# Sparse attention and slot experts on one core: GpSimd lowers the scores of batch 0 one group later and ends the new threshold, and ScalarE's sign passes follow

## The reference

```python
def sparsemax(z):
    z_sorted = -jnp.sort(-z, axis=-1)
    cum = jnp.cumsum(z_sorted, axis=-1)
    k = jnp.arange(1, S + 1, dtype=z.dtype)
    support = 1.0 + k * z_sorted > cum
    k_sup = jnp.sum(support, axis=-1, keepdims=True)
    cum_sel = jnp.take_along_axis(cum, k_sup - 1, axis=-1)
    tau = (cum_sel - 1.0) / k_sup
    return jnp.maximum(z - tau, 0.0)
```

## Time and profile before

| | us |
|---|---|
| median of 3 runs | 485.32 (484.76 to 485.77) |
| the profiled execution | 485.12 |
| its span | 483.4 |
| VectorE busy | 313.0 (65%) |
| TensorE busy | 400.4 (83%) |
| ScalarE busy | 225.9 (47%) |
| GpSimd busy | 149.1 (31%) |

### The profile page before, as it was taken

One profiled execution on the slowest core, in us unless ns is written; L12 is line 12 of the kernel. 1 busy time (PEld: TensorE's weight loads), 2 busy tenths in 40 slices (PEclk: granted clock), 3 DMA queues, 4 the chain that ended last, 5 costly groups with the idle time before them and its releaser, 6 DMA issues. The chain is left out here.

```text
span 483.4 us, 6967 instructions
## 1 busy us (share of the span) xinstructions
PE 400.4 (83%) x2091; PEld 248.0 (51%) x2091; DVE 313.0 (65%) x1189; ACT 225.9 (47%) x412; POOL 149.1 (31%) x243
## 2 busy tenths in 40 slices
PE   3886576778897987997888998999997659999983
PEld 3543223234454554565656775734443326888872
DVE  3699999978999986675214244333332214989996
ACT  2226647646686796788434654200000001346671
POOL 3105645554858523333111110010000000335453
PEclk9997888788999998999997999999999799999998
DMA  4294011010010128458228757649999999901125
GB/s 148 86 296 131 10 44 43 1 43 27 19 43 2 62 103 298 130 182 295 90 87 301 264 176 241 255 140 392 392 395 394 393 379 356 356 5 45 55 77 174
DMA packets 44030, 83.78 MB, mean 173 GB/s; under 512 B 1878, under 2 KB 36316, under 8 KB 39388
## 3 DMA queue, kind: packets, MB, share of 16 engines
q1 hardware_dynamic: 42936, 82.15, 48.3%
q10 hardware_dynamic: 1060, 1.22, 0.8%
HBM read 70.78 MB, written 12.58 MB: 172 GB/s over the span
## 5 line engine op out<-in xcount | busy, mean ns | idle before, releaser
L1071 PE MATMUL bank<-Wz,yT 128*128 128x512 f32 x128 | 70.8, 706 | 25.9 <-DVE top L1649 23.3
L1071 PEld LDWEIGHTS bank<-Wz,yT 128*128 128x128 f32 x128 | 28.0, 228 | 61.5 <-issue 50.3
L1649 DVE MAX8 top<-bank 128x8 f32<-128x32 f32 x512 | 51.5, 180 | 1.9 <-ACT arena L746 1.7
L1007 ACT ACTIVATE d<-d 128x32 f32<-128x32 f32 x16 | 3.7, 230 | 89.4 <-DVE d L2029 89.4
L579 POOL TENSOR_SCALAR veps<-mv 128x4 f32<-128x4 f32 x24 | 5.9, 244 | 108.8 <-DVE mv L1577 76.4
L1104 PE MATMUL bank<-aWo,hoT 128*128 128x256 f32 x128 | 37.0, 413 | 0.1
L687 POOL TENSOR_TENSOR work<-work 128x512 f32<-128x512 f32 x16 | 16.6, 1058 | 64.7 <-DVE work L2104 64.7
L1138 PE MATMUL bank<-arena,Wd 128*128 128x512 f32 x64 | 29.2, 599 | 3.2 <-ACT arena L809 3.2
L1167 PE MATMUL bank<-d,work 128*128 128x256 f32 x128 | 30.6, 385 | 0.9 <-ACT d L837 0.9
L1509 PE MATMUL bank<-scr,work 128*128 128x256 f32 x128 | 29.1, 381 | 1.6 <-ACT work L1020 1.6
L1485 PE MATMUL bank<-scr,arena 128*128 128x256 f32 x128 | 28.9, 381 | 0.0
(11 more groups left out here) (267 smaller groups left out, 880.3 us busy)
## 6 DMA issues: line engine op xcount, KB each, us to landing
arena<-in_L_ffn_e_W_dram SPq DMA_DIRECT2D x10, 1024.0 KB, 7.8
x<-in_L_ffn_e_W_dram SPq DMA_DIRECT2D x9, 1024.0 KB, 9.4
arena<-in_L_ffn_e_Wg_dram SPq DMA_DIRECT2D x7, 1024.0 KB, 11.3
scr<-in_L_ffn_e_W_dram SPq DMA_DIRECT2D x7, 1024.0 KB, 13.8
work<-in_L_ffn_e_W_dram SPq DMA_DIRECT2D x5, 1024.0 KB, 14.0
xin<-in_L_attn_query_dram SPq DMA_DIRECT2D x8, 512.0 KB, 4.1
x<-in_L_attn_query_dram SPq DMA_DIRECT2D x1, 4096.0 KB, 16.5
out_dram<-x SPq DMA_DIRECT2D x8, 512.0 KB, 5.5
```

What stands on the lines that cost most here:

```text
L1071: mm = pe.matmul(bZ[t % 2][:, :], yT[:, c, t * P:(t + 1) * P], Wz[:, c, :], start=(c == 0), stop=(c == C - 1))
L1649: mx = v.max(top[:, h * TG + t, :], bZ[t % 2][:, h * NS:(h + 1) * NS])
```

## The change

- GpSimd: `lower(i)` of batch 0 moves behind `subtract(i+1)` (the last one stays behind `new_threshold(3)`). A new GpSimd function `new_threshold` does exc - 1 when the sum is there, multiplies it with VectorE's reciprocal and adds `tau`: three 128x64 instructions. VectorE's L1698 and L1704 go in batch 0. Two of the three steps replace those, the third is the split of a combined one.
- VectorE waits for `tau_ready` before it overwrites `tau` (L1663).
- ScalarE: `signs(i)` moves one group later, to the place behind `clamp(i+1)` and `mark(i+1)`; it writes to `unread`, a free stretch of `arena`, and no longer to `above`. The order behind it is now `put_scores(i+1, 2:4)`, `norm_y(i+2)`, `put_yT(i+2)`, `put_scores(i+2, 0:2)`: `norm_y` has changed places with `put_scores(i+1, 2:4)`.
- TensorE's, SyncE's orders and batch 1 are as before, apart from counted semaphore values.

```diff
--- before.py
+++ after.py
@@ -133,6 +133,7 @@
         y = sb("y", [P, TG, D])
         yT = sb("yT", [P, C, GT])
         d = sb("d", [P, TG * 512])
+        unread = arena[:, 12288:13312].bitcast(BF16)
         above = sb("above", [P, TG * 512], BF16)
         top = sb("top", [P, HR, TOP])
         tau = sb("tau", [P, HR])
@@ -256,6 +257,7 @@
         found = sem("found")
         fix = sem("fix")
         tau_ready = sem("tau_ready")
+        risen = sem("risen")
         lowered = sem("lowered")
         signed = sem("signed")
         settled = sem("settled")
@@ -327,6 +329,7 @@
         psH = bank[6][:, 0:D]
         psO = bank[7][:, 0:D]
         N_W2, N_W3 = 7, 3
+        NW = 6
 
         (M_MISC, M_AQ, M_KQ, M_WZ, M_DK, M_DQ, M_V, M_WD) = range(1, 9)
         PREP = M_WD
@@ -596,7 +599,8 @@
 
             def lower(i, b):
 
-                hold(tau_ready, i + 1)
+                pool.wait_ge(tau_ready, i + 1)
+                pool.nop(nofuse=True)
                 z3 = scr[b][:, :, bass.ds(i * TG - b * KT, TG), :]
                 pool.tensor_tensor(z3, z3, tauf[:, :].rearrange("p (h t) -> p h t", h=NH).unsqueeze(3)
                                    .broadcast_to([P, NH, TG, NS]), ALU.subtract).then_inc(lowered, 1)
@@ -611,6 +615,16 @@
                                        tau[:, :].rearrange("p (h t) -> p h t", h=NH)[:, h, :].unsqueeze(3)
                                        .broadcast_to([P, NH // 2, TG, NS]), ALU.subtract).then_inc(diff, 1)
 
+            def new_threshold(i):
+
+                hold(newton, i * (NW - 1) + 1)
+                pool.tensor_scalar(tauf[:, :], exc[:, :], -1.0, None, ALU.add).then_inc(risen, 1)
+                hold(newton, i * (NW - 1) + 4)
+                pool.wait_ge(risen, i * 2 + 1)
+                pool.tensor_tensor(tauf[:, :], tauf[:, :], rcnt[:, :], ALU.mult).then_inc(risen, 1)
+                pool.wait_ge(risen, i * 2 + 2)
+                pool.tensor_tensor(tauf[:, :], tau[:, :], tauf[:, :], ALU.add).then_inc(tau_ready, 1)
+
             def slot_root(b):
                 pool.wait_ge(smean, 2 * b + 2)
                 pool.tensor_scalar(sveps[:, :], smv[:, 1:2], EPS, None, ALU.add).then_inc(srst, 1)
@@ -619,12 +633,14 @@
 
             roots(0, 0)
             roots(0, 1)
-            with pool.Fori(0, GB - 1) as i:
+            subtract(0, 0)
+            roots(0, 2)
+            new_threshold(0)
+            with pool.Fori(1, GB) as i:
                 subtract(i, 0)
+                lower(i - 1, 0)
                 roots(0, i + 2)
-                lower(i, 0)
-            subtract(GB - 1, 0)
-            roots(0, GB + 1)
+                new_threshold(i)
             lower(GB - 1, 0)
 
             pool.wait_ge(dve_part, PREP)
@@ -766,7 +782,7 @@
             def signs(i, b):
 
                 act.wait_ge(lowered, i + 1)
-                act.activation(above[:, :].rearrange("p (h t s) -> p h t s", h=NH, t=TG),
+                act.activation((unread if b == 0 else above)[:, :].rearrange("p (h t s) -> p h t s", h=NH, t=TG),
                                scr[b][:, :, bass.ds(i * TG - b * KT, TG), :], ACT.Sign, bias=tiny[:, 0:1],
                                accum_out=ahead[:, bass.ds(i, 1)]).then_inc(signed, 1)
 
@@ -844,26 +860,21 @@
             put_scores(0, 0, range(TG))
             put_yT(1)
             put_scores(1, 0, range(2))
-            with act.Fori(0, GB - 2) as i:
+            for i in range(GB - 1):
                 clamp(i)
                 mark(i)
+                if i > 0:
+                    signs(i - 1, 0)
+                put_scores(i + 1, 0, range(2, TG))
                 norm_y(i + 2)
-                put_scores(i + 1, 0, range(2, TG))
                 put_yT(i + 2)
-                put_scores(i + 2, 0, range(2))
-                signs(i, 0)
-            clamp(2)
-            mark(2)
-            norm_y(4)
-            put_scores(3, 0, range(2, TG))
-            put_yT(4)
-            put_scores(4, 1, range(2))
-            signs(2, 0)
+                put_scores(i + 2, (i + 2) // GB, range(2))
 
             clamp(3)
             mark(3)
+            signs(2, 0)
+            put_scores(4, 1, range(2, TG))
             norm_y(5)
-            put_scores(4, 1, range(2, TG))
             put_yT(5)
             signs(3, 0)
             put_scores(5, 1, range(2))
@@ -1660,13 +1671,16 @@
                                        in1=rk[:, :].unsqueeze(1).broadcast_to([P, HR, TOP]),
                                        op0=ALU.add, op1=ALU.mult).then_inc(cum, 1)
                 v.wait_ge(cum, i * 3 + 2)
+                if not (isinstance(i, int) and i in (0, GB + 1, GB + 2, GB + 3)):
+
+                    v.wait_ge(tau_ready, i)
                 v.tensor_reduce(tau[:, :], top[:, :, :], AX_X, ALU.max).then_inc(cum, 1)
 
             def scores_at(i, b):
                 return scr[b][:, :, bass.ds(i * TG - b * KT, TG), :]
 
             def steps_ahead(i, b):
-                return i * NW if b == 0 else GB * NW + (i - GB) * (NW + 1)
+                return i * (NW - 1) if b == 0 else GB * (NW - 1) + (i - GB) * (NW + 1)
 
             def count(i, b, marks):
 
@@ -1688,12 +1702,14 @@
                 v.wait_ge(folded, 2 * i + 2)
                 v.tensor_reduce(cnt[:, :], a2[:, :, 0:NS // 4], AX_X, ALU.add).then_inc(newton, 1)
 
-            def new_threshold(i, at):
+            def new_threshold(i, at, by_pool=False):
 
                 v.wait_ge(newton, at)
                 v.tensor_scalar(cnt[:, :], cnt[:, :], 1.0, None, ALU.max).then_inc(newton, 1)
                 v.wait_ge(newton, at + 1)
                 v.reciprocal(rcnt[:, :], cnt[:, :]).then_inc(newton, 1)
+                if by_pool:
+                    return
                 v.wait_ge(newton, at + 2)
                 v.scalar_tensor_tensor(out=rcnt[:, :], in0=exc[:, :], scalar=-1.0, in1=rcnt[:, :],
                                        op0=ALU.add, op1=ALU.mult).then_inc(newton, 1)
@@ -1705,7 +1721,7 @@
 
             def settle(i, b, marks):
 
-                new_threshold(i, steps_ahead(i, b) + (2 if marks else 3))
+                new_threshold(i, steps_ahead(i, b) + (2 if marks else 3), by_pool=marks)
                 v.tensor_reduce(tot[:, 0, bass.ds(i - b * GB, 1)], cnt[:, :], AX_X, ALU.add).then_inc(newton, 1)
 
             def half_rows(a, u):
@@ -1738,7 +1754,7 @@
             def check(b):
 
                 n = GB + b
-                v.wait_ge(newton, steps_ahead(GB * (b + 1) - 1, b) + NW + b)
+                v.wait_ge(newton, steps_ahead(GB * (b + 1) - 1, b) + (NW - 1, NW + 1)[b])
                 v.wait_ge(signed, GB * (b + 1) + b)
                 if b == 0:
                     v.tensor_scalar(tot[:, 1, 0:GB], ahead[:, 0:GB], float(HR * NS), 0.5, ALU.add, ALU.mult)\
@@ -1910,7 +1926,6 @@
                     v.tensor_copy(hidT[:, :, b, :], bZ[1][:, 32:64].rearrange("p (c e) -> p c e", c=C)).then_inc(dve_part, 1)
                     v.wait_ge(slots, s0 + NSL)
 
-            NW = 6
             NSL = 8
             first_statistics(1)
             v.wait_ge(bo_in, 32)
```

## The result

The changed kernel takes 492.75 us (median of 4 runs, 492.43 to 494.31) against 485.04 (4 runs, 484.53 to 485.77). The ratio is 1.0163, 95% interval 1.0141 to 1.0185: 7.7 us or 1.6% slower. Forecast were 487.0 and a range up to 489.6, so the sign was right, the size too small by a factor of four, and the time lies outside the range. The profiled execution took 492.43, its span is 490.7.

A forecast was written before the change was run, and what follows sets the result against it. VectorE bounds batch 0 before; afterwards a ScalarE-TensorE loop of 11.88 + D does. The last pair ends at 88.08 + 4D = 107.88 against 106.09, 1.8 us later: 487.0 us, range 484.6 to 489.6.

The forecast's parts named there:

- The chain: Batch 0, ScalarE and TensorE: serial steps from one group's clamp to the next, last pair 1.8 us later.
- closing pair D: TensorE, a group's last score products, for the next group but one: 4.95 us each, bounds 3.70 and 6.54.
- the turn: TensorE's turn of y between norm_y and put_yT, taken from 80.15 to 81.38 us.
- What bounds the kernel: Before the change, batch 0 goes at VectorE's pace; the last score pair's end, 106.09 us, releases batch 1 through the check.
- VectorE's part: VectorE in batch 0: 0.52 us a group saved by dropping L1698 and L1704, scan 0.32 shorter in groups 0 to 2.
- The fold: VectorE's fold, groups 1 to 3: waits 0.4 us for GpSimd's lowering, taking back the scan's 0.32.
- GpSimd's three instructions: GpSimd's 128x64 threshold steps in batch 0: 0.25 us each, hidden beside VectorE's sort.
- The loop 11.88 + D: ScalarE and TensorE, clamp to clamp in batch 0: 11.88 us plus the closing score pair, 16.83 us in all.
- The bound: TensorE's upper limit for a closing pair: 6.54 us, taken as a pair wholly at half clock.
- 88.08: Batch 0: the fixed part, in us, of the forecast end of the last closing pair, 88.08 + 4D = 107.88.
- Granted clock over batch 0: TensorE's granted clock in batch 0: would be lower than 0.80.
- Late xin: Load of xin lands at 54.2 us in group 0, against group 1's statistics wanted at about 53.3; 0.9 late once.

The follow-up runs named there:

- experiment 11: Changed kernel with VectorE's last two threshold steps (L1698, L1704) back and GpSimd's three small instructions out in batch 0: 493.28 us, ratio 1.0197 to the kernel before.
- experiment 12: Kernel before with only norm_y(i+2) moved behind the copies of put_scores(i+1, 2:4) in ScalarE's order: 493.50 us, ratio 1.0197.
- experiment 1: Changed kernel with ScalarE's sign pass moved from behind the mark to behind put_yT: 487.82 us, ratio 1.0058 to the kernel before.
- experiment 3: Changed kernel with 16 idle products ahead of each turn of y in batch 0 and 4 behind it: 484.20 us, ratio 0.9987 to the kernel before.
- experiment 2: Changed kernel with sign pass behind put_yT, norm_y directly behind the mark and GpSimd's roots ahead of the lowering: 488.44 us, ratio 1.0068 to the kernel before.
- experiment 4: Kernel before with only the new threshold's last steps moved to GpSimd, L1698 and L1704 out of VectorE: 483.93 us, ratio 0.9996.

## Why the prediction was wrong in size

The chain was the right one, and the sign came out by it and not by luck. The step that failed is TensorE's part of the chain: the closing pair D was taken at 4.95 us and took 6.00 on average, and the turn was taken at full clock, 1.23 us, and took 1.98 three times in four. Point by point:

- **What bounds the kernel, and that the end of the last closing pair is the number to follow**: right. Flag minus pair end was 2.39 before and 2.38 after; the pair's end moved by 7.2 and the span by 7.3.
- **VectorE's part**: right. 0.52 us a group (L1725 at 64.16, 0.47 behind the reciprocal), scans of 1.22, 1.23, 1.22, and one of 2.56 beside the last lowering. The fold did not wait in the changed kernel, since the late clamp put it behind the lowering's end.
- **GpSimd's three instructions**: 0.38 to 0.68, 0.32 and 0.32 us, above my 0.25, and hidden (experiment 11 finds no cost).
- **The loop 11.88 + D**: the right mechanism and nearly the right length. Clamp to clamp is 19.13 us (57.30 to 76.43) and 18.11 (76.43 to 94.54). With the measured D of 6.55 and 5.52, 11.88 + D gives 18.43 and 17.40; the rest, 0.70 and 0.71, is in the main the turn at half clock (1.98 for 1.23). What the prediction says of the cause is half right: of the things that "stand ahead of `norm_y`" now, the sign pass had been in the loop before (experiment 12), and only the two copies are new in it. It never worked out the loop of the kernel before, 10.86 + D with 0.95 us of slack.
- **D and the turn, the step that failed.** "I take 4.95, which lies nearer to 5.37 than to 3.70 as the idle time suggests." Measured were 5.22, 6.55, 5.52 and 6.70, together 23.99 against 19.80: 4.2 us. Three turns at half clock, which the prediction took at full clock, are another 2.2. The rest, -0.9, is that group 0's score copy came at 46.54 in place of 47.43 although the stretch began 0.5 later, since the pair of products ahead of it took 5.22 in place of 6.54. 88.08 + 23.99 + 2.2 = 114.3, less 0.9 = 113.4; the trace has 113.30.
- The mean over the four pairs of before was the wrong average: it held pairs of a TensorE that waits 1.3 to 2.2 us ahead of them (the one of 3.70 stood behind 1.26 us of idling, not directly behind other products), and the change made waits of 4.92, 4.99 and 4.95 ahead of the turns. The bound was misread too: the pair of 6.54 was not wholly at half clock, the granted clock over it was 0.56. Twice 3.70 is 7.4, and one pair of the changed kernel took 6.70, above the bound.
- No row of before gives the right centre. Behind the same 4.5 us of idling one pair took 6.54 in the kernel before, 5.22 in the changed kernel and 6.71 in experiment 1. With 6.54 for all four and the turn at full clock the sum is 88.08 + 4 x 6.54 = 114.2, near the trace's 113.30, but by chance: with the turns as they were it is 116.5.
- **Granted clock over batch 0**: forecast lower than 0.80. It was: 0.78 in the changed kernel from 36.66 to the last pair's end at 113.30, against 0.80 in the kernel before from 36.66 to 106.09. The mean moved little, because the half speed moved more than it grew: the pairs of products ahead of the turns, 5.10 to 5.17 in groups 1 to 3 of the kernel before, take 3.67 in groups 1 and 3 now, and the pairs and turns that the loop waits for take longer.
- **Late xin**: not where I looked for it. The statistics of group 1 began at 53.32 without a wait, since group 0's score copy and with it `norm_y` came 0.9 earlier. It was late by 0.38 and 0.30 us in groups 2 and 3, where the loop was later still, and by more once the clock was up (experiment 3).

What stays open: how much of the clock's misplacement is due to the order and how much to the moment at which stretches of half speed fall (5.22, 6.54 and 6.71 us behind equal waits). The sum explains this trace; for other executions only the times (492.43 to 494.31) are known.

## What to carry to other kernels

Before you reorder an engine's queue, write down the chain from an instruction of a group to the same instruction of the next group, through every engine, with everything that stands in the queue between, and compare its length with the period; an engine that is busy 10.98 of 19.13 us, as ScalarE was here, can still close such a loop. Do it for the kernel before too: its slack, 0.95 us here, is what a reordering may use up. Price every step of TensorE in the loop by the clock behind the waits that the new order makes, not by the mean of the old, and give the range the slowest such step on record, since equal waits gave 5.22 to 6.71. And when work is taken off the bounding engine, ask what the freed instructions will meet: here the scan met the lowering.

## What the runs showed of the hardware

VectorE instructions with two SBUF inputs and a GpSimd instruction that reads SBUF excluded each other. The scan: 1.22 us alone, 1.54 to 2.72 beside the lowering, always ending 1.07 to 1.08 behind the lowering's end. The fold: 1.14 alone, 3.35 beside it. It goes the other way too: GpSimd's first small instruction took 0.38 us when it began behind VectorE's fold (63.37 in the changed kernel) and 0.68 when it began beside the fold (45.05, 80.91, 99.01). A reduction beside the same lowering: 2.29, as ever. That is the rule of the Trainium skill (SBUF — State Buffer, "Who interferes with whom"), and the trace agrees. The prediction gave it 0.4 us; in experiment 2 it cost 2.2 us in each of groups 1 to 3, and in experiment 4 it took back in the profiled execution what VectorE saved.

Twenty idle products a group in TensorE's waits raised the granted clock in batch 0 from 0.78 (36.66 to 113.30) to 0.95 (36.66 to 105) and shortened a kernel bound by a chain of short steps by 8.5 us, although not one instruction of the chain was removed.
